# Expert logits taken from unnormalised rows, with the layer norm applied to the logits and the normalised rows made after the list of experts

## The reference, cut to what matters

```
x = x + gnn_branch(xn, ...) + linear_attention(xn, w_qkv, w_proj, b_proj)
x = x + ffn(layernorm(x), Wg, bg, W1, b1, W2, b2)

layernorm(x) = (x - mean(x)) / sqrt(var(x) + 1e-5)          # by row
ffn:  logits = layernorm(x) @ Wg + bg                        # (625, 8)
      the two largest logits of each row, softmax over the two -> comb (625, 8)
      x += sum over experts e of comb[:, e] * (silu(xe @ W1[e] + b1[e]) @ W2[e] + b2[e])
```

## Time and profile before

| | |
|---|---|
| median of 3 runs | 845.24 us (845.07 to 846.45) |
| the profiled execution: its own time | 843.48 us |
| the profiled execution: span from first to last instruction | 841.7 us |
| PE busy, share of the span | 800.7 us, 95% |
| DVE busy | 539.5 us, 64% |
| ACT busy | 248.6 us, 30% |
| POOL busy | 148.2 us, 18% |

### The profile page before, as it was taken

The page is one execution under the profiler, slowest core; times in us unless marked ns, Lnnn a source line. Parts: engine busy times, 40 slices in busy tenths (PEclk is TensorE's granted clock), DMA queues, the critical chain, the costliest instruction groups (busy, mean ns, idle before and its releaser), DMA issues.

```text
span 841.7 us, 10823 instructions
## 1 busy us (share of the span) xinstructions
PE 800.7 (95%) x3995; PEld 640.9 (76%) x3995; DVE 539.5 (64%) x743; ACT 248.6 (30%) x468; POOL 148.2 (18%) x96
## 2 busy tenths in 40 slices
PE   4999999999999999999998999997699999999997
PEld 3988766847477777765767778897598888888886
DVE  5876998979989999999777426068541111511112
ACT  4252223316411013222045332142432321432310
POOL 2011001120100000002201350031343330433300
PEclk9999999999999998999999999999589999999999
DMA  7533779796878768742041120000242120322001
GB/s 245 213 50 47 227 214 337 266 276 158 240 228 276 246 220 282 242 139 100 1 159 58 48 97 1 1 2 1 100 151 96 55 98 2 100 100 100 0 0 61
DMA packets 64211, 110.21 MB, mean 131 GB/s; under 512 B 6815, under 2 KB 16412, under 8 KB 64172
## 3 DMA queue, kind: packets, MB, share of 16 engines
q1 hardware_dynamic: 54476, 96.71, 34.5%
q0 software_dynamic: 6912, 7.70, 5.4%
q10 hardware_dynamic: 2784, 5.27, 1.7%
HBM read 105.81 MB, written 1.28 MB: 127 GB/s over the span
## 4 chain that ended last, share of the span: by engine, by line
PE 89%; DVE 6%; issue 2%; ACT 1%; POOL 1%; DVEq 0%; POOLq 0%
PE bank L1310 55%; PE bank L1730 13%; PE bank L1396 6%; PE bank L1511 4%; PE bank L1528 3%; PE bank L1522 2%; PE bank L1505 2%; PE bank L1326 1%; DVE st L890 1%; PE bank L1437 1%; PE bank L1333 1%; DVE slot L987 1%; ACT slot L581 1%; DVE slot L885 0%; DVE slot L1116 0%
## 5 line engine op out<-in xcount | busy, mean ns | idle before, releaser
L1004 DVE SCALAR_TENSOR_TENSOR weights<-weights,att 128x2048 f32<-128x2048 f32 x116 | 268.9, 2392 | 2.7 <-DMA weights<-in_L_gnn_basis 2.1
L1291 DVE CAST hid_hi<-slot 128x626 fp32r<-128x626 f32 x32 | 15.6, 487 | 160.7 <-ACT slot L846 160.7
L1310 PE MATMUL bank<-half,ew_hi 128*128 128x314 f32 (+1 forms) x512 | 114.0, 312 | 2.2 <-POOL ew_lo L550 2.2
L1310 PE MATMUL bank<-AT,slot 125*128 125x312 f32 (+1 forms) x400 | 105.9, 426 | 0.8 <-ACT slot L711 0.8
L1310 PEld LDWEIGHTS bank<-AT,slot 125*128 125x128 f32 x400 | 75.5, 189 | 31.0 <-ACT slot L711 1.0
L550 POOL TENSOR_TENSOR ew_lo<-weights,ew_hi 128x1024 fp32r<-128x1024 f32 x28 | 69.4, 2500 | 134.4 <-ACT ew_hi L828 134.4
L1310 PEld LDWEIGHTS bank<-half,ew_hi 128*128 128x128 f32 x512 | 88.4, 193 | 5.6 <-issue 2.9
L581 ACT ACTIVATE slot<-bank 128x312 f32<-128x312 f32 (+6 forms) x88 | 43.8, 525 | 148.7 <-PE bank L1310 128.9
L1310 PE MATMUL bank<-weights,slot 128*125 128x512 f32 (+5 forms) x306 | 86.9, 447 | 0.3 <-ACT slot L581 0.3
L846 ACT ACTIVATE slot<-bank,eb_now 128x312 f32<-128x312 f32 x64 | 33.3, 522 | 157.2 <-PE bank L1310 157.2
L1310 PE MATMUL bank<-half,ew_lo 128*128 128x312 f32 (+1 forms) x256 | 79.5, 310 | 0.0
(11 more groups left out here) (297 smaller groups left out, 1116.4 us busy)
## 6 DMA issues: line engine op xcount, KB each, us to landing
weights<-in_L_gnn_basis SPq DMA_DIRECT2D x60, 1024.0 KB, 5.5
weights<-in_L_ffn_W SPq DMA_DIRECT2D x32, 512.0 KB, 4.5
weights<-in_L_mix_kqv_w SPq DMA_DIRECT2D x1, 3072.0 KB, 10.2
weights<-in_w_qkvT SPq DMA_DIRECT2D x3, 1024.0 KB, 5.4
slot<-slot POOLq DMA_DIRECT2D x10, 250.0 KB, 6.5
weights<-in_L_mix_mlp_w ACTq DMA_DIRECT2D x2, 1024.0 KB, 13.6
weights<-in_L_gnn_root ACTq DMA_DIRECT2D x2, 1024.0 KB, 8.7
slot<-in_row_mlp_b POOLq DMA_DIRECT2D x1, 1250.0 KB, 26.1
```

Source lines behind the costliest of these rows:

```text
L1004: ins = dve.scalar_tensor_tensor(wrel[layer][r], wmat(at), att[:, layer, r, b:b + 1], wrel[layer][r], ALU.mult, ALU.add)
L1310: ins = pe.matmul(out, a, b, start=i == 0, stop=i == len(pairs) - 1)
```

## The change

The logits come from rows as they are. With m and r the mean of a row and the reciprocal of its deviation, `layernorm(x) @ Wg` is `r * (x @ Wg - m * sum(Wg))`. So the kernel

- makes `sum(Wg)` over the 512 features once, on PE, from a matrix of ones (`es`, between `atT` and `xkv`, earlier in the layer), and DVE copies it out (`wg_sum`);
- has PE transpose the tiles of `x` itself (`xrT`), ACT copy them once each, and PE make the logits from these;
- has DVE add the tiles to `x` and take their statistics (the normalisation between them is gone), with one square root and one reciprocal for all five tiles;
- has DVE work out `m * sum(Wg)` ahead of the logits, subtract it, multiply by r, and add the bias, three instructions where one was;
- puts the five normalisations on DVE behind the list of experts, and behind these the transposes `xeT` on PE, both copies on ACT and the remainder `xe_lo` on POOL. On DVE the work towards `comb` stands behind the normalisations.

Core of the diff:

```diff
-              ("kv", 3), ("qfT", 4), ("xk", 5), ("at", 2), ("xv", 5), ("atT", 1), ("xkv", 1), ("ha", 1),
+              ("kv", 3), ("qfT", 4), ("xk", 5), ("at", 2), ("xv", 5), ("atT", 1), ("es", 1), ("xkv", 1), ("ha", 1),
-              ("xeT", 5), ("el", 1), ("en", 1), ("combT", 2), ("eb2", 5), ("eh", 3)]
+              ("xrT", 5), ("el", 1), ("en", 1), ("xeT", 5), ("combT", 2), ("eb2", 5), ("eh", 3)]
...
# ACT
-            for j in range(TT + 1):
-                if j < TT:
-                    sqrt_of_tile("xe_row", 0, j)
-                if j:
-                    tile = B("xeT", j - 1)[:, 0:KT * P].rearrange("p (k t) -> p k t", k=KT)
-                    act.wait_ge(S("psum_full"), filled("xeT", j))
-                    act.activation(col(2)[:, :, P * j - P:P * j], tile, ACT.Copy).then_inc(S("xe_col"), 1)
-                    copy_out("xeT", j - 1, xe_hi[:, :, P * j - P:P * j], tile)
+            for j in range(TT):
+                copy_out("xrT", j, col(2)[:, :, P * j:P * j + P], B("xrT", j)[:, 0:KT * P].rearrange("p (k t) -> p k t", k=KT))
+            act.wait_ge(S("xe_row_var"), 1)
+            act.activation(sd[0:P, :], mv[0:P, :, 1:2].rearrange("p j o -> p (j o)"), ACT.Sqrt, bias=eps[0:P, 0:1]).then_inc(S("xe_row_std"), 1)
             act.wait_ge(S("gap"), 3)
             act.activation(eexp, eexp, ACT.Exp).then_inc(S("gap_exp"), 1)
             link(act.activation(small[0:1, 1010:1011], eps[0:1, 0:1], ACT.Silu))
+            for j in range(TT):
+                tile = B("xeT", j)[:, 0:KT * P].rearrange("p (k t) -> p k t", k=KT)
+                act.wait_ge(S("psum_full"), filled("xeT", j + 1))
+                act.activation(col(2)[:, :, P * j:P * j + P], tile, ACT.Copy).then_inc(S("xe_col"), 1)
+                copy_out("xeT", j, xe_hi[:, :, P * j:P * j + P], tile)
...
# DVE
+            dve.wait_ge(S("psum_full"), filled("es", 1))
+            dve.tensor_copy(wg_sum, B("es")[0:P, 0:E1]).then_inc(S("es_out"), 1)
...
-            layernorm_by_tile(x, row(1), "xe_row", x3_row)
+            for j in range(2):
+                x3_row(j)
+                x3_statistics(j)
+            for j in range(2, TT):
+                x3_row(j)
+            for j in range(2, TT):
+                ins = x3_statistics(j)
+            ins.then_inc(S("xe_row_var"), 1)
...
+            dve.tensor_tensor(U[1], x3_mean, wg_sum.unsqueeze(1).to_broadcast([P, TT, E1]), ALU.mult)
+            dve.wait_ge(S("xe_row_std"), 1)
+            link(dve.reciprocal(rs[0:P, :], sd[0:P, :]))
...
+            dve.tensor_tensor(U[0], B("el")[0:P, 0:TT * E1].rearrange("p (j e) -> p j e", j=TT), U[1], ALU.subtract).then_inc(S("el_out"), 1)
             dve.wait_ge(S("el_out"), 1)
+            link(dve.tensor_tensor(U[0], U[0], bc(rs[0:P, :], E1), ALU.mult))
+            link(dve.tensor_tensor(U[0], U[0], small[0:P, 0:E1].unsqueeze(1).to_broadcast([P, TT, E1]), ALU.add))
...
             dve.tensor_copy(el_i[0:1, 8:9], key1[:, 0:1]).then_inc(S("elist"), 1)
+            for j in range(TT):
+                dve.tensor_scalar(row(1)[:, j, :], x[:, j, :], mv[0:P, j, 0:1], rs[0:P, j:j + 1], ALU.subtract, ALU.mult).then_inc(S("xe_row"), 1)
             one_hots(U[0], E1, U[2:4], idx)
...
# PE
+            bk = claim(pe, "es")
+            pe.wait_ge(S("Wg_in"), 32)
+            group(bk[0:P, 0:E1], [(ones[:, 0:P], Wg[:, k, :]) for k in range(KT)]).then_inc(S("psum_full"), 1)
...
             def expert_logits(j):
-                pe.wait_ge(S("xe_col"), j + 1)
+                pe.wait_ge(S("act_read"), READ0["xrT"] + j + 1)
...
-                tile_to_cols("xeT", j, j, row(1), "xe_row")
+                tile_to_cols("xrT", j, j, x, "x3r_out")
...
             group(bk[0:1, 0:E1], [(ones[0:P, 0:1], table(6, 5, E1)...)]).then_inc(S("psum_full"), 1)
+            for j in range(TT):
+                tile_to_cols("xeT", j, j, row(1), "xe_row")
             pe.wait_ge(S("comb"), 1)
```

More of the change, by code:

```diff
@@ L98 @@
              ("xn2A", 12), ("aq", 1), ("ak", 1), ("av", 1), ("ad", 1), ("uk", 8), ("xbw", 5), ("uq", 8), ("conv", 8),
[1 row of a table removed]
+             ("kv", 3), ("qfT", 4), ("xv", 5), ("atT", 1), ("ha", 1), ("xo", 8), ("xrT", 5), ("xeT", 5), ("combT", 2)]
 READ0, _at = {}, 0
@@ L283, in gps_two_layers @@
         hv = small[0:P, 988:993]
+        wg_sum = small[0:P, 100:100 + E1]
         x_sum, x_mean = small[0:P, 976:981], small[0:P, 981:986]
@@ L1234, in x3_row, with x3_statistics @@
                 dve.tensor_tensor(x[:, j, :], B("xpr", X3_TILE[j])[0:P, :], x[:, j, :], ALU.add).then_inc(S("x3r_out"), 1)
+            def x3_statistics(j):
                 dve.wait_ge(S("x3r_out"), j + 1)
-            layernorm_by_tile(x, row(1), "xe_row", x3_row)
-            U = [table(6, i, E1) for i in range(6)]
+                link(dve.bn_stats(st[0:P, j, :], x[:, j, :]))
+                return dve.bn_aggr(mv[0:P, j, :], st[0:P, j, :])
+            for j in range(2):
[6 more added lines that the diff above has]
+            ins.then_inc(S("xe_row_var"), 1)
+            U = [table(6, i, E1) for i in range(6)]
+            x3_mean = mv[0:P, :, 0:1].to_broadcast([P, TT, E1])
+            dve.wait_ge(S("xe_row_var"), 1)
+            dve.tensor_tensor(U[1], x3_mean, wg_sum.unsqueeze(1).to_broadcast([P, TT, E1]), ALU.mult)
+            dve.wait_ge(S("xe_row_std"), 1)
+            link(dve.reciprocal(rs[0:P, :], sd[0:P, :]))
             dve.wait_ge(S("psum_full"), filled("el", 1))
             dve.wait_ge(S("Wg_in"), 32)
-            dve.tensor_tensor(U[0], B("el")[0:P, 0:TT * E1].rearrange("p (j e) -> p j e", j=TT),
-                              small[0:P, 0:E1].unsqueeze(1).to_broadcast([P, TT, E1]), ALU.add).then_inc(S("el_out"), 1)
+            dve.tensor_tensor(U[0], B("el")[0:P, 0:TT * E1].rearrange("p (j e) -> p j e", j=TT), U[1], ALU.subtract).then_inc(S("el_out"), 1)
             dve.wait_ge(S("el_out"), 1)
+            link(dve.tensor_tensor(U[0], U[0], bc(rs[0:P, :], E1), ALU.mult))
+            link(dve.tensor_tensor(U[0], U[0], small[0:P, 0:E1].unsqueeze(1).to_broadcast([P, TT, E1]), ALU.add))
             largest(U[0])
@@ L1690, in expert_logits @@
             def expert_logits(j):
-                pe.wait_ge(S("xe_col"), j + 1)
+                pe.wait_ge(S("act_read"), READ0["xrT"] + j + 1)
                 return group(B("el")[0:P, E1 * j:E1 * j + E1], [(col(2)[:, k, P * j:P * j + P], Wg[:, k, :]) for k in range(KT)])
-            pe.wait_ge(S("Wg_in"), 32)
             for j in range(TT):
-                tile_to_cols("xeT", j, j, row(1), "xe_row")
+                tile_to_cols("xrT", j, j, x, "x3r_out")
                 if j == 1:
```

## The result

The changed kernel takes 848.03 us (median of 20 runs, 846.07 to 851.17) against 845.04 us of the kernel before (median of 20 runs, 840.93 to 846.58). The ratio of the two kernels is 1.0047, with a 95% interval of 1.0032 to 1.0062: slower by about 4 us, somewhere between 2.7 and 5.2. The ratio goes by all runs and not by the two medians alone: the medians differ by 2.99 us, the means of the twenty runs by 3.98. The profiled execution took 849.36 us, span 847.6. Single executions of either kernel spread over 5 us and bunch around two values some 3 us apart, so a median moves with how many fall where, and from one pair of profiles only the stages can be compared, each from its own first instruction.

A forecast was written before the change was run, and what follows sets the result against it. The chain from logits over the list to POOL's first weight remainder and the expert matmuls was taken as the bound. -2.65 + 0.45 + 0.6 + 7.3 = +5.7 us gave 850.9 us, range 846.0 to 853.0.

The forecast's parts named there:

- the rival in which POOL's queue acts alone: List to experts: DVE slips between POOL's instructions at no loss, `comb` 5.8 us behind the list; +1.5, 846.7 us; chance 0.22.
- the sum: Whole kernel: -2.65 + 0.45 + 0.6 + 7.3 = +5.7 us, giving 850.9 us.
- Up to the logits, -2.65: Stage before the list: transposing raw rows avoids waits for normalisation, so logits come 2.65 us earlier, with PE's clock falling at 589.5.
- Two more instructions behind the logits, +0.45: DVE behind the logits: multiply by the reciprocal deviation and add the bias, 0.21 us size, 0.23 each with hand-over; +0.45 us.
- The sum of Wg, +0.6: PE before `xkv`: eight weight loads and 8-column matmuls, 0.95 us, less 0.34 of PE idle time; +0.6 us.
- From the list to the experts, +7.3: L is the completed list: POOL's remainders and held DVE put `comb` at L + 10.3, experts at L + 16.95 against L + 9.64.
- The hold: Behind the list: POOL's running instructions block DVE's, about one DVE instruction passing per POOL instruction; `comb` at 10.3 instead of 5.8.
- The start of the experts, 0 with ±1: From the first expert matmul: the clock's rise behind the start shifts the half-clock loss, now 2.94 us, by ±1.
- The rival of a clock that stays: PE from 589.5 on: clock stays at 1.0, last logits take 3.0 instead of 6.0 us; -1.3, 843.9 us; chance 0.06.
- That the change does nothing behind the list: List to experts: all moved work hides under the weight fetch, 9.64 us stays; -1.6, 843.6 us; chance 0.05.
- The rival of more than the sum: Behind the list: DVE passed over by POOL, or later instructions also held by the split; +7 to +9, 853 us; chance 0.07.

The follow-up runs named there:

- the one with fillers: Changed kernel plus matmuls nobody reads on PE, 12 ahead of `comb` and 8 ahead of the expert loop: 846.07 us, ratio 1.0022 to the kernel before.
- the best: Changed kernel, normalisations in DVE's idle time, POOL waiting for `comb`, two tiles' columns ahead of the list, two remainders on POOL, three on DVE: 839.98 us, ratio 0.9951.
- the kernel with `comb` first: Changed kernel with the five normalisations put behind the work towards `comb` on DVE: 844.91 us (10 runs), ratio 1.0016 to the kernel before.
- the one with both edits: Changed kernel with normalisations in DVE's idle time ahead of the logits and POOL waiting for `comb` ahead of its remainders: 844.84 us, ratio 0.9994.

## Why the prediction was right, point by point

The time fell in the range (848.03 in 846.0 to 853.0) and on the forecast side; the mechanism is the one forecast. The time alone wouldn't have told it: 848.03 is nearer to the 846.7 of the rival in which POOL's queue acts alone than to the 850.9 of the sum, and only the stages and the experiments decide between them. The sum, +5.7 us, was larger than the ratio's +4.0 and lies above its interval (2.7 to 5.2).

- *Up to the logits, -2.65:* the mechanism is right, the size depends on the clock. From the norm to the reading of the logits it took 30.69 and 30.76 us in the two profiles with the old order, and 25.19 to 28.09 in the ten with the new one. In the two with the old order the clock fell 22.1 and 22.0 us behind the norm. Where it fell at the same distance with the new order, at 22.1 us (the kernel in which POOL waits), it took 27.50, so the part of the change is -3.2 at an equal clock. Where it fell a little earlier, at 21.5 to 21.9 us, it took 27.7 to 28.1; at 22.8 to 22.9 (the change and the one with fillers) 26.8, and at 24.8, 25.2. In the sum I took the clock's fall as fixed at one place. I also counted 1.40 us at full clock for a tile's logits and the next transposes (0.95 + 0.45), where in the change the weight loads of the first three groups of logits start 1.25 us apart (590.29, 591.54 and 592.80). That step was mis-sized by 0.6 us at equal clock, by 1.2 in the pair of profiles.
- *Two more instructions behind the logits, +0.45:* 3.50 against 3.02, right.
- *The sum of Wg, +0.6:* +0.27, shown by itself. A listed length of PE was taken for its cost.
- *From the list to the experts, +7.3:* +7.0. POOL from L + 3.0 (2.98), its five to L + 9.25 (9.04), DVE held (five instructions, each to one of POOL's ends), `comb` at L + 10.3 (10.0), then 6.65 (6.66). The sum has a slip of 0.1 here: 9.25 and 1.15 make 10.4. And the forecast had the cast as the first to be held. It wasn't: normalising took 2.35 us, not up to 2.75, so the cast came at the very start of POOL's work (604.38, POOL from 604.36) and took its 0.17, as it did in the kernel with fillers (604.98, POOL from 604.94). Whether it slipped in ahead or would have passed a busy POOL, 0.02 us don't tell. In its place line 1294 was held, so that there were five all the same and less was left behind the fifth. The hold is shown by three edits: with POOL's rows removed, with POOL merely later, and with normalisations earlier.
- *The start of the experts, 0 with ±1:* -1.32 in this pair. From the first expert matmul to the end the profiles run from 229.56 to 230.90; the four longest have the clock rising 5.8 to 6.1 us behind the start, the two shortest 3.1 and 3.3. Over the ten kernels with the new order the mean is 230.1, the two with the old are 230.9 and 230.8. From that I estimate about -0.7; with two profiles of the old order, and single ones 1.3 apart, it isn't shown.

With the measured sizes at equal clock, 0.27 - 3.2 + 0.48 + 7.0 = +4.55, and with the estimate of -0.7 for the experts' start, +3.9, close to the ratio's 4.0. The rival of POOL's queue alone (+1.5) falls by the lengths of DVE's instructions. The rival of a clock that stays falls too: it was at 0.50 from 593.9 on, though it fell later than forecast. That the change does nothing behind the list is refuted by L + 16.66. The rival of more than the sum falls as well: behind POOL's fifth nothing was held (line 1295 took 0.19), and POOL's split started only when `comb` stood.

Where did the gain go? The logits come 3 to 4 us earlier, as meant. But the rows had been normalised, turned over and split while PE made the logits, mostly under its work. Behind the list the same instructions lie in front of the first expert weights on POOL, next to DVE's work towards `comb`. That stands at L + 10 instead of L + 3, 2.3 us of it by the normalisations and 4.7 by the hold. The versions that keep the earlier logits, let POOL wait and share the remainders between POOL and DVE are faster than both kernels: 0.5% (0.34 to 0.64%) under the kernel before in the best. The others (only the wait, only the normalisations moved to either place, wait and normalisations together, all remainders on DVE) are not told from the kernel before.

## What to carry to other kernels

Work that is taken off a chain is not gone: look at what runs beside it in its new place, and where several engines work in a pipeline look first at POOL and DVE, which here took turns one instruction for one, so that tiny DVE instructions cost as much as POOL's large ones. A chain of small DVE instructions should run before POOL starts, even if POOL has to wait for it, as the added wait showed (experts 2.7 us earlier). And if an engine idles for a result (here DVE for the logits), that hole takes the work that was to be put behind.

## What the runs showed of the hardware beyond the forecast

- POOL and DVE hold each other in both directions: with two of the remainders on DVE, POOL's three took 4.55 us instead of 3.7, and DVE's two 2.46 instead of the 1.3 that the first two take when POOL is idle (3.03 for all five). The Trainium skill ("SBUF — State Buffer", section "SBUF: two separate sides") says that the pair of ports is taken for a whole instruction by whichever comes first; both lengths agree with it. A RECIPROCAL of DVE, one small input, kept its 0.19 us beside a busy POOL each time, while a TENSOR_SCALAR of the same 125x5 was held (1.14 and 1.24 us instead of 0.17).
- Transposes alone can raise PE's clock. In the kernel with the remainders on DVE PE had nothing but transposes from 599.1 until the clock rose. Its windows:

```profile
600.00:601.00 1.00, 1.00 (x7) 0.50 0.82 196
...
603.00:604.00 1.00, 0.65 (x4) 0.50 1.04 307
604.00:605.00 1.00, 1.00 (x5) 0.59 1.05 360
605.00:606.00 1.00, 0.24 (x2) 1.00 1.04 387
```

The clock went up to 1.0 near 604.8, behind 20 transposes of 125x125 back to back (599.1 to 603.5) and during the 5 of `comb` (603.8 to 605.0). It rose at such a place also where POOL waits (603.7), in the kernel with `comb` first (611.1), in the one with both edits (605.6) and in the one with two remainders on DVE (602.3). But it didn't in the change itself and in the kernel with only the normalisations moved, with the same 20 transposes (602.0 to 606.4 and 595.9 to 600.4). The forecast cited the Trainium skill ("TensorE: Matmul & The Clock Gate", section "Part 4: PE-mode transpose") for transposes not counting as work; these rows contradict that for this kernel's fp32 transposes, and the measurement decides. What tells the kernels apart in which it rose stays open.
